# State-space projection: four batches in two separated pairs, against one line of 24 blocks

## The reference

```python
proj = hidden_states @ W_in * mup_vector
z, xBC, dt = jnp.split(proj, [D_SSM, D_SSM + CONV_DIM], axis=-1)
conv = conv_b + sum((conv_w[:, k] * xp[:, k:k + L] for k in range(K)))
xBC = silu(conv)                       # x (512), Bm (128), Cm (128)
dt = softplus(dt + dt_bias)
dA = exp(dt * (-exp(A_log)))
state = state * dA + (dt * x) * Bm;  y = state . Cm + D * x
out = rmsnorm(y * silu(z)) * norm_w @ W_out
```

## Time and profile before

| | before |
|---|---|
| median of 3 runs | 1563.83 us (1562.64 to 1567.59) |
| the profiled execution | 1557.24 us, its span 1555.5 us |
| mean granted clock of TensorE | 0.897 |
| TensorE, matmuls | 1230.6 us (79%) |
| VectorE | 1003.2 us (64%) |
| ScalarE | 617.3 us (40%) |
| GpSimd | 621.2 us (40%) |

### The profile page before, as it was taken

How to read it: one execution, slowest core, us unless ns; L and a number is a source line. 1 busy time by engine, 2 the same in 40 slices (tenths; PEclk the granted TensorE clock), 3 DMA queues, 4 the chain that set the end, 5 groups by cost and what they waited for, 6 DMA issues and landing times. The chain is left out here.

```text
span 1555.5 us, 35259 instructions
## 1 busy us (share of the span) xinstructions
PE 1230.6 (79%) x13688; PEld 936.0 (60%) x13688; DVE 1003.2 (64%) x2108; ACT 617.3 (40%) x1380; POOL 621.2 (40%) x540
## 2 busy tenths in 40 slices
PE   1789898989844999994456869888888846999992
PEld 1356665656533989883223436666666634898882
DVE  5478898888865555465586555766666465554565
ACT  4357676666641333342455631121111132333341
POOL 0245445454502333232304345775757502333322
PEclk8799999999965999997578968999999966999997
DMA  4656656666425976643100000000000036967634
GB/s 147 146 136 160 182 166 159 175 162 168 126 60 221 421 289 234 249 163 122 54 1 14 1 14 2 2 3 2 3 2 2 2 83 271 421 247 257 220 142 172
DMA packets 93701, 209.89 MB, mean 135 GB/s; under 512 B 33058, under 2 KB 64547, under 8 KB 87395
## 3 DMA queue, kind: packets, MB, share of 16 engines
q1 hardware_dynamic: 83938, 185.11, 36.4%
q0 software_dynamic: 7488, 20.46, 3.8%
q10 hardware_dynamic: 2112, 2.10, 0.4%
HBM read 152.84 MB, written 37.49 MB: 122 GB/s over the span
## 5 line engine op out<-in xcount | busy, mean ns | idle before, releaser
L1221 ACT ACTIVATE ffn_h<-ffn_bank,ffn_b 128x256 f32<-128x256 f32 (+1 forms) x384 | 144.7, 431 | 271.7 <-PE ffn_bank L117 268.6
L2190 POOL TENSOR_TENSOR ssm_GL<-ssm_L,ssml_G 128x512 f32<-128x512 f32 x128 | 164.9, 1298 | 109.5 <-DVE ssm_L L2099 109.5
L1398 DVE CAST ffn_hh<-ffn_h 128x512 f16<-128x512 f32 (+1 forms) x192 | 73.1, 381 | 185.9 <-ACT ffn_h L1221 185.1
L1033 POOL DMA_INDIRECT ffn_xs<-xn_rows,ffn_from_rows x78 | 78.5, 1007 | 271.2 <-PE ffn_bank L1116 184.7
L115 PE MATMUL ffn_bank<-ffn_hh,ffn_W 128*128 128x256 f16 (+1 forms) x768 | 180.2, 253 | 5.2 <-DVE ffn_hl L1400 5.0
L116 PE MATMUL ffn_bank<-ffn_hl,ffn_W 128*128 128x256 f16 (+1 forms) x768 | 180.0, 252 | 0.0
L117 PE MATMUL ffn_bank<-ffn_hh,ffn_W 128*128 128x256 f16 (+1 forms) x768 | 180.0, 252 | 0.0
L1955 PE MATMUL ssm_Y<-ssm_GL,ssmh_windows 64*32 64x64 f32 x4096 | 145.9, 224 | 8.6 <-POOL ssm_GL L2190 8.2
L2099 DVE TENSOR_TENSOR_SCAN ssm_L<-ssm_bank,ssmh_ident 128x512 f32<-128x512 f32 x128 | 151.2, 1209 | 1.7 <-PE ssm_bank L1938 1.6
L1955 PEld LDWEIGHTS ssm_Y<-ssm_GL,ssmh_windows 64*32 64x32 f32 x4096 | 125.0, 111 | 37.4 <-issue 25.8
L641 ACT ACTIVATE att_prob<-att_bank,att_nmax 128x512 f32<-128x512 f32 (+3 forms) x256 | 127.4, 526 | 29.8 <-DVE att_nmax L723 28.5
(11 more groups left out here) (348 smaller groups left out, 3186.3 us busy)
## 6 DMA issues: line engine op xcount, KB each, us to landing
ffn_W<-split_w SPq DMA_DIRECT2D x46, 2048.0 KB, 10.4
att_piece<-in_ffn_w SPq DMA_DIRECT2D x32, 512.0 KB, 5.4
split_w<-att_halves SPq DMA_DIRECT2D x32, 512.0 KB, 4.4
att_Q<-att_pair SPq DMA_DIRECT2D x64, 128.0 KB, 2.4
ffn_back<-y_rows SPq DMA_DIRECT2D x16, 512.0 KB, 7.2
att_KB<-att_krl SPq DMA_DIRECT2D x8, 512.0 KB, 5.5
att_Q<-att_pair SPq DMA_DIRECT2D x64, 64.0 KB, 2.1
xn_rows<-ffn_XN SPq DMA_DIRECT2D x8, 512.0 KB, 2.6
```

The costliest lines, as they stand in the source:

```text
L1221: ins_ = act.activation(h[layer][:, m, 0:n], bank[1 + 2 * layer + u][:, (m % 2) * n:(m % 2 + 1) * n], ACT.Gelu, bias=bias[:, ds(e + m, 1)])
L2190: pool.tensor_tensor(GL[:, p % RING, :, :, :].rearrange("p x i n -> p x (i n)"), L[:, p % RING, :, :, :].rearrange("p x i n -> p x (i n)") ...
```

## The change

The four batches become one line of 24 blocks, written out on each engine, with no loop and no separate turning. The first two products of the next batch stand before the turn of x, and that turn is cut in two halves, the second behind the next batch's first gate; ScalarE's copies and its last skip of a batch move along. The softplus becomes a polynomial of degree 10 in e, one step after each of the blocks 0 to 10; the decays follow after blocks 13 to 15. The turns stand inside batches 2 and 3, all over banks 5 and 6, and the turn of x in batch 3 waits until the last of them is copied. The scratch lies in the rows of batch 3 alone, and `starts` has a tile of its own. In the diff `(b, c)` and `(b, n)` are batch and block.

```diff
+LOG_SERIES = (1.0, -0.4999990165233612, ..., -0.0032440233044326305)
...
+        starts = sb("starts", [P, PAIRS * S])
+        last = NT - TB
+        u, e, dA, dT = two(zs, 0), two(zs, 2), two(zs, 2), two(skip, 0)
+        suffix, ends, Ftok = [three(dtx, 0), three(skip, 1)], two(dtx, 0), starts[:, :]
...
+            def turn_x(b, half):
+                pe.wait_ge(s["silu"], (b + 1) * CB)
+                if b == 2:
+                    pe.wait_ge(s["turned"], 2 * PAIRS)
+                if b == 3:
+                    pe.wait_ge(s["turned"], 5 * PAIRS)
+                for i in (2 * half, 2 * half + 1):
...
-            pe.wait_ge(s["turned"], 5 * PAIRS)
-            with pe.Fori(B // 2, B) as b:
-                project(b)
+            for b in range(B):
+                for c in range(XB):
+                    conv_block(b, c + 2)
+                    gate(b, c)
+                    if c == 0 and b:
+                        turn_x(b - 1, 1)
+                    if c == 1:
+                        turn_b(b)
+                    if c == 2:
+                        multiply_g(b)
+                    if (b, c) == (2, 1):
+                        pe.wait_ge(s["dt_done"], 1)
+                        turn(lambda r, i: dT[:, r * S + i * P:r * S + (i + 1) * P], 0, 2 * TB)
+                    if (b, c) == (2, 2):
+                        pe.wait_ge(s["ft_done"], 1)
+                        turn(lambda r, i: FT[:, r, i * P:(i + 1) * P], PAIRS, 2 * TB)
+                    if (b, c) == (3, 1):
+                        pe.wait_ge(s["suffix_done"], 1)
+                        turn(lambda r, i: ends[:, (r * TB + i) * P:(r * TB + i + 1) * P], 2 * PAIRS, 3 * TB)
+                    if (b, c) == (3, 2):
+                        spread_ends(0)
+                    if (b, c) == (3, 3):
+                        spread_ends(1)
+                if b + 1 < B:
+                    conv_block(b + 1, 0)
+                    conv_block(b + 1, 1)
+                turn_x(b, 0)
+            turn_x(B - 1, 1)
...
+            for N in range(NB):
+                b, n = divmod(N, CB)
+                if n == 0 and b:
+                    keep_x(b - 1, 0)
+                    keep_x(b - 1, 1)
+                if n == 1 and b:
+                    keep_x(b - 1, 2)
+                    keep_x(b - 1, 3)
+                if N + 2 < NB:
+                    first_tap(N + 2)
+                silu(N)
+                if n < XB:
+                    gate(b, n)
+                if n == 0 and b:
+                    skipped(b - 1, XB - 1)
+                if n > 2:
+                    skipped(b, n - 3)
...
+                if (b, n) == (2, 0):
+                    act.wait_ge(s["dt_done"], 1)
+                    act.activation(dA, dT, ACT.Exp, scale=neg_a[:, :]).then_inc(s["da_done"], 1)
+                if (b, n) == (2, 2):
+                    turned(lambda r: dtt[:, 2 * r:2 * r + 2, :, :], 0, TB)
+                if (b, n) == (2, 4):
...
+                if (b, n) == (3, 2):
+                    turned(lambda r: Etok[:, 2 * r:2 * r + 2, :, :], 2 * PAIRS, TB)
+                if (b, n) == (3, 4):
+                    decay_rows(0)
+            skipped(B - 1, XB - 1)
+            decay_rows(1)
+            for i in range(TB):
+                keep_x(B - 1, i)
...
-                steps(dve.reciprocal(zz, zz))
...
+                steps(dve.tensor_scalar(dT, e, LOG_SERIES[-1], None, ALU.mult))
                 yield
+                for term in LOG_SERIES[-2::-1]:
+                    steps(dve.scalar_tensor_tensor(dT, dT, term, e, ALU.add, ALU.mult))
+                    yield
+                dve.wait_ge(s["dt_u"], 1)
+                dve.tensor_tensor(dT, dT, u, ALU.add).then_inc(s["dt_done"], 1)
                 yield
...
+            def decays():
                 yield
+                yield
                 dve.wait_ge(s["da_done"], 1)
...
+                dve.tensor_scalar(flat(hi16), dA, 1.0 / UNSCALE, None, ALU.mult).then_inc(s["hi_done"], 1)
...
+            work = itertools.chain(softplus(), decays())
+            for b in range(B):
                 for n in range(CB):
                     sum_taps(b, n)
                     next(work, None)
...
+            pool.memset(suffix[0][:, :, CH - 1:], 1.0)
             wait_alone(pool, s["da_done"], 1, s["passed"])
+            wait_alone(pool, s["turn_psum"], PAIRS, s["passed"])
+            pool.memset(suffix[1][:, :, CH - 1:], 1.0)
...
-            wait_alone(pool, s["turned"], 5 * PAIRS, s["passed"])
+            wait_alone(pool, s["turned"], PAIRS, s["passed"])
```

More of the change, by code:

```diff
@@ L1526, in ssm_project_stage @@
         dtt = sb("dtt", [P, B, TB, SH])
[L1528 to L1535, removed]
+        starts = sb("starts", [P, PAIRS * S])
+        last = NT - TB
+        two = lambda a, at: a[:, last + at:last + at + 2, :].rearrange("p a n -> p (a n)")
+        three = lambda a, at: (a[:, last + at:last + at + 3, :].rearrange("p a n -> p (a n)").rearrange("p (c n) -> p c n", c=NC))
+        u, e, dA, dT = two(zs, 0), two(zs, 2), two(zs, 2), two(skip, 0)
+        suffix, ends, Ftok = [three(dtx, 0), three(skip, 1)], two(dtx, 0), starts[:, :]
         bank = t.banks()
@@ L1556, in _ @@
                                        bb == 0 and k == 0, bb == 1 and k == KD - 1)
                 ins.then_inc(s["dt_psum"], 1)
[L1559 to L1609, removed]
-                for i in range(TB):
@@ new lines, in turn_b, with multiply_g @@
+            def turn_b(b):
+                pe.wait_ge(s["silu"], b * CB + 1)
+                pe.wait_ge(s["g_done"], b + 1)
+                for i in range(TB):
+                    ins = pe.transpose(bank[7][:, i * P:(i + 1) * P], bc[:, i * P:(i + 1) * P], identf[:, :])
+                ins.then_inc(s["b_psum"], 1)
+            def multiply_g(b):
+                pe.wait_ge(s["silu"], b * CB + 2)
+                pe.wait_ge(s["b_done"], b + 1)
+                for i in range(TB):
+                    one = slice(i * P, (i + 1) * P)
+                    ins = pe.matmul(bank[7][:, one], bc[:, one], CT[:, b * TB + i, :], start=True, stop=True)
+                ins.then_inc(s["g_psum"], 1)
@@ L1614, in project, with turn @@
                     ins.then_inc(s["xt_psum"], 1)
-            def turn(rows, bks, chunks):
+            def turn(rows, before, chunks_read):
+                pe.wait_ge(s["xt_done"], 2 + chunks_read)
+                pe.wait_ge(s["turned"], before)
                 for r in range(PAIRS):
-                    for i in range(chunks):
-                        ins = pe.transpose(bank[bks[r]][:, i * P:(i + 1) * P], rows(r, i), identf[:, :])
+                    for i in range(TB):
+                        ins = pe.transpose(bank[5 + r][:, i * P:(i + 1) * P], rows(r, i), identf[:, :])
@@ L1635, in _, with spread_ends @@
[L1635 to L1639, removed]
+            def spread_ends(par):
+                pe.wait_ge(s["turned"], (3 + par) * PAIRS)
                 end = par * CH + CH - 1
                 for r in range(PAIRS):
-                    pe.matmul(bank[5 + r if par == 0 else 1 + r][:, :], identf[:, end:end + 1].broadcast_to([P, P]),
-                              Ftok[:, r * S:(r + 1) * S], start=True, stop=True).then_inc(s["turn_psum"], 1)
@@ L1658, in _, with first_tap, silu @@
             act.activation(u, u, ACT.Relu).then_inc(s["dt_u"], 1)
-            def turned(out, bks, first, chunks):
+            def first_tap(N):
+                b, n = divmod(N, CB)
+                act.wait_ge(s["conv_psum"], N + 1)
+                if N >= 3:
+                    act.wait_ge(s["silu"], N - 2)
+                act.activation(taps[:, n % 3, :], bank[n % 3][:, :], ACT.Copy, scale=conv_w[:, ORDER[n], SK - 1:SK]).then_inc(s["copied"], 1)
+            def silu(N):
+                b, n = divmod(N, CB)
+                act.wait_ge(s["tapped"], N + 4)
+                c = ORDER[n]
+                if n == 0:
+                    if b:
+                        act.wait_ge(s["g_psum"], b)
+                    out = bc[:, :]
+                elif n == 1:
+                    out = CT[:, b * TB:(b + 1) * TB, :].rearrange("p a n -> p (a n)")
+                else:
+                    if b:
+                        act.wait_ge(s["xt_psum"], b * TB)
+                    out = xc[:, c, :]
+                act.activation(out, taps[:, n % 3, :], ACT.Silu, bias=conv_b[:, c:c + 1]).then_inc(s["silu"], 1)
@@ new lines, in skipped, with gate @@
+            def skipped(b, c):
+                act.wait_ge(s["silu"], b * CB + c + 3)
+                if b == B - 1 and c == 0:
+                    act.wait_ge(s["turn_psum"], PAIRS)
+                if b == B - 1 and c == 1:
+                    act.wait_ge(s["suffix_done"], 1)
+                act.activation(skip[:, b * XB + c, :], xc[:, c, :], ACT.Copy, scale=d_col[:, c:c + 1])
+            def gate(b, i):
+                act.wait_ge(s["z_psum"], b * TB + i + 1)
+                if b == B - 1 and i == 0:
```

(35 more changed lines are left out.)

113 lines of the change are left out of this document (60 added, 53 removed).

## The result

The median went from 1563.75 us to 1538.0 us (four runs each, 1533.86 to 1543.96 after); the ratio is 0.9835, 95% interval 0.9806 to 0.9864, so 21 to 30 us. A second measurement of the same kernel gave 0.9821 (0.9790 to 0.9852); each ratio is to runs of the kernel before that were taken beside it. The profiled execution has a span of 1532.1 us.

The account below looks back on a forecast made before the run. No engine is full in the stage; they wait on each other. Gains of 24.2 us up to block 11 and 6.3 after make 30.5, less 1.5 for clock falls: 1563.8 - 29 = 1535 us, range 1529 to 1549.

Parts of the forecast that it names:

- Start: Zeroing of `starts` (0.91 us) moves behind the dt weights on VectorE; first tap sum from 780.15 to 779.25.
- Softplus: Batches 0 and 1: 3.52 us per block with its step, block 11 ends at 819.6 instead of 843.8, gaining 24.2 us.
- The cover: Under softplus, turning x takes 4.7 us while VectorE holds 8.2 us of work; 3.5 us spare, 2 at low clock.
- Batch 2: VectorE waits 3.5 us for Exp, scan takes 2.42 (bounds 2.4 and 4.0), tap sum 14 at 833.0, 17 at 844.3.
- GpSimd: Suffix products end at 845.9 to 848, TensorE asks at 853.3, so nothing waits; rival of GpSimd late, 1540, chance 0.05.
- Batch 3: Silu 23 at 868.5, last skip 869.9, second spread's copies end at 871.0, and only then is x turned.
- The term of 1.5 us for falls: Allowance for TensorE's clock falling after pauses, some 2.6 us per fall where TensorE leads; bounds 0 and 13.
- Tail: Turning x waits 1.1 us for spread copies, then 6.3 us to the last weighing as in old batch 2; end 877.3.
- What follows the stage: Next stage's entry unchanged, priced at nothing; 3 us if its slow-clock stretch ended a pair or two earlier or later.
- the clock did fall often: Rival: four to six clock falls, two thirds on the path, 8 to 15 us lost, 1542 to 1549; chance 0.21.
- the slow side: Rival: clock stuck at the 1.2 GHz level through the stage, 13 us slower, 1577; chance 0.03.
- The rival of a still shorter stage: Batches 2 and 3 run at TensorE's 16.1 us each, stage ends at 870, total 1527; chance 0.08.

Follow-up runs that it names:

- filled: Changed kernel plus 10, 12 and 9 spare matmuls in TensorE's waits before turning FT, x of batch 2 and the first spread; stage 113.2 us, ratio 0.9824.
- both_filled: Changed kernel with later turns and later decays, plus 12 matmuls before the turn of x of batch 2 and 10 before the second spread; stage 104.6 us, ratio 0.9752.
- other_banks_filled: Later turns and decays, second spread in banks 7 and 3, plus 12 matmuls before the turn of x of batch 2; stage 103.0 us, ratio 0.9744.
- other_banks: Later turns and decays, second spread in banks 7 and 3, x of batch 3 turned right after the last silu; stage 103.1 us, ratio 0.9741.
- pool_early: Changed kernel with dt in the tile of the turned dt and GpSimd's suffix products begun after Exp, beside the scan; stage 112.3 us, ratio 0.9818.
- line_old_log: Changed kernel with the old series for the softplus, a piece after each of blocks 0 to 10; stage 124.7 us, ratio 0.9911.

## Why the prediction was right

The forecast was 1535 (29 less), the measurement 1538.0 (25.8 less, 21 to 30), and the stage alone 28.0 less, against 30.5 in the sum before the clock.

- **Start**: first tap 0.87 us earlier from the stage's start (14.45, now 13.58); forecast 0.9.
- **Softplus**: on my axis (3.45 taken off) block 11 ended at 819.2; forecast 819.6. The cover held: there is no idle time on VectorE from 782.73 to 827.16, so the turn of x was in time.
- **Batch 2**: wait for Exp 3.77 (forecast 3.5), scan 2.29 (2.42), block 14 at 832.3 (833.0), block 17 at 843.3 (844.3).
- **GpSimd**: done at 846.2 on that axis (845.9 to 848); asked for at 855.3 (853.3). No rival here.
- **Batch 3**: here the sum was short. Last silu begins at 871.4 on my axis (867.9), x turned from 874.2 (871.0). Nearly all of it is the clock, 3.1 us by the filled kernel. The term of 1.5 us for falls was too small by half, and it was a guess in both its parts. I priced a fall at 2.6 us, which I had read from no row; three cost 3.1, so about 1.0 each. And I expected less than one on the path, where three came. Two of their places I had named, inside batch 2 and at x(2); the third was the first spread, after a pause of 1.97, while the second spread, which I had named, saw none after 3.48.
- **Tail**: the new wait for the spread's copies was priced at 1.1; the pair both_filled and other_banks_filled shows 1.6 for it at full clock. From the turn of x to the last weighing it took 5.6 us in place of 6.3. The 6.3 was read from batch 2 of the kernel before, whose turn of x ran at the low clock (3.85); here it ran at full clock. So the stage's end is 2.5 late where x is 3.2 late.
- **The total**: the interval of 21 to 30 us holds the 29 of the forecast and the 28.0 of the stage, so the 3 us between 1535 and 1538 say nothing of the mechanism. That the stage itself is only 1.0 off is in part luck: misses in both directions cancelled, block 17 being 1.0 early, the last silu 3.5 late and the tail 0.7 shorter, against a clock term of 1.5.
- **What follows the stage**: priced at nothing, and so it was. From the last weighing to the last addition of this layer's output it took 344.5 us in both kernels, and 37.5 of the first 60 us were at the low clock in both.
- **The rivals**: the clock did fall often, but three times and for 3 us, not 8 to 15; GpSimd was not late; the slow side never came near, since the clock was 0.93 over the stage where it was 0.82. The rival of a still shorter stage had its end at 870 and was wrong for this kernel (879.8), but not out of reach: counted from the same start, other_banks ends at 868.8.

What I did not see before: a product standing behind a wait for copies. I followed the queues and wrote down the waits, but took them as given; moved, they are worth 6.7 us of the stage, the falls of the clock behind them included.

## What to carry to other kernels

Where two kinds of work wait for each other's ends, put one piece of the one behind each piece of the other and count which engine is then full: the gain is the idle time, and it can be worked out from the queue of that engine. In a queue worked in order, put an instruction that waits for another engine's copy behind the products that could run meanwhile; here that was worth 6.7 us, a quarter of what the whole change gave. Measure a local change by its stage: stages that nobody touched moved the total by several us from one execution to the next.

## What the runs showed of the hardware

- Pauses of 1.97 to 2.86 us of TensorE were followed by stretches at the 1.2 GHz level, but not always: pauses of 2.41 and 1.97 at two of these places in pool_early were not, nor was the one of 3.48 in the changed kernel. The length of a pause alone does not tell; what else decides stays open.
- With its pauses filled with spare matmuls TensorE kept 2.4 GHz. In filled, which left the pause before the second spread, the clock fell there instead; in both_filled, with the later turns and the pause between the spreads filled too, it stayed at 1.00 to within 1 us of the stage's end.
- The scan of 128x1024 took 2.29 us with only the start of a memset of GpSimd's beside it, 2.94 where a copy of GpSimd's had begun 0.22 us ahead of it, and 3.99 where a product of 1.90 had begun 0.05 ahead.
- Of the next stage's first 60 us, 37.5 ran at the low clock in both kernels, but 17.0 in line_old_log, 18.5 in other_banks_filled and 29.1 in filled. From 8 us after the stage's end, TensorE was busy all of the time that it spent at the low clock. The time from the last weighing to the layer's last addition (340.8 to 348.0 us over all runs) does not follow from that share alone: 344.1 with 17.0 and 340.8 with 18.5. What decides it stays open; it blurs totals by more than the small edits here are worth.
